# Last stage of a two-layer kernel: the routing weights of 48 of 64 experts spread by DMA, in four pieces a tile

## What is computed

```python
x = x + _L0_attn_ref(_layernorm(x), ...)       # selective mixing, 16 states
x = x + _L0_ffn_ref(_layernorm(x), ...)        # 9 experts, top 2
x = x + _L1_attn_ref(_layernorm(x), ...)       # 16 heads, causal, 256 tokens a row
x = x + _L1_ffn_ref(_layernorm(x), ...)        # 64 experts, top 8

def _L1_ffn_ref(x, centroids, expert_biases, Ws_up, Ws_down, W_up, W_down):
    shared = silu(xf @ Ws_up) @ Ws_down
    aff = xf @ centroids.T
    _, idx = top_k(aff + expert_biases, 8)
    w = sigmoid(take_along_axis(aff, idx, axis=1))
    w = w / (sum(w, axis=-1, keepdims=True) + 1e-08)
    cw = zeros((T, 64)).at[arange(T)[:, None], idx].add(w)
    h = silu(einsum('td,edf->etf', xf, W_up))     # 64 experts, 128 -> 64
    y = einsum('etf,efd->etd', h, W_down)         # 64 -> 128
    return shared + einsum('etd,te->td', y, cw)
```

## Time and profile before

| | us |
|---|---|
| median of 3 runs | 1128.03 (1126.86 to 1128.64) |
| the profiled execution | 1126.31 |
| its span | 1124.5 |
| TensorE busy | 981.0 (87%) |
| VectorE busy | 846.1 (75%) |
| ScalarE busy | 723.8 (64%) |
| GpSimd busy | 439.8 (39%) |

### The profile page before, as it was taken

One profiled execution on the slowest core, in us unless ns is written; L12 is line 12 of the kernel. 1 busy time (PEld: TensorE's weight loads), 2 busy tenths in 40 slices (PEclk: granted clock), 3 DMA queues, 4 the chain that ended last, 5 costly groups with the idle time before them and its releaser, 6 DMA issues.

```text
span 1124.5 us, 20697 instructions
## 1 busy us (share of the span) xinstructions
PE 981.0 (87%) x6164; PEld 779.5 (69%) x6164; DVE 846.1 (75%) x1938; ACT 723.8 (64%) x1416; POOL 439.8 (39%) x503
## 2 busy tenths in 40 slices
PE   5665089999658999999999989999999999999998
PEld 3444079999536777776776667777777677777776
DVE  4865577777568888888887667878787768787865
ACT  4543045555347778778777667777777667777775
POOL 0266750000156556555553303333333333333343
PEclk9555589999869999999999989999999999999999
DMA  9011122222211101101010013241414140505050
GB/s 251 18 45 46 65 58 65 64 66 66 68 28 24 34 20 29 29 23 36 20 30 11 1 43 86 50 87 44 92 36 101 35 103 12 124 12 125 12 124 10
DMA packets 59749, 61.68 MB, mean 55 GB/s; under 512 B 15973, under 2 KB 54022, under 8 KB 57606
## 3 DMA queue, kind: packets, MB, share of 16 engines
q1 hardware_dynamic: 54976, 52.02, 19.4%
q0 software_dynamic: 4096, 8.40, 2.4%
q10 hardware_dynamic: 582, 0.09, 0.0%
HBM read 45.73 MB, written 14.75 MB: 54 GB/s over the span
## 4 chain that ended last, share of the span: by engine, by line
PE 74%; DVE 12%; ACT 5%; issue 5%; POOL 1%; DMA 1%; SPq 1%; DVEq 0%; POOLq 0%; ACTq 0%
PE ps L2070 5%; PE ps L2048 5%; PE ps L2050 4%; PE ps L2049 4%; PE ps L2072 4%; PE ps L2071 4%; PE ps L1848 4%; PE ps L1791 3%; PE ps L1911 3%; PE ps L2057 3%; PE ps L1866 3%; PE ps L1894 3%; PE ps L1872 2%; PE ps L1770 2%; PE ps L1769 2%
## 5 line engine op out<-in xcount | busy, mean ns | idle before, releaser
L741 POOL TENSOR_TENSOR hl<-h,hh 128x512 fp32r<-128x512 f32 x128 | 165.7, 1294 | 309.0 <-ACT hh L1017 309.0
L1017 ACT ACTIVATE hh<-h 128x512 fp32r<-128x512 f32 (+1 forms) x264 | 165.0, 625 | 17.4 <-DVE h L1634 16.1
L1534 DVE TENSOR_REDUCE nm<-ps 128x4 f32<-128x512 f32 (+1 forms) x128 | 116.3, 951 | 35.6 <-PE ps L1894 33.7
L1634 DVE TENSOR_TENSOR h<-sg,ps 128x512 f32<-128x512 f32 x160 | 108.2, 676 | 39.5 <-ACT sg L1005 37.9
L1005 ACT ACTIVATE sg<-ps 128x512 f32<-128x512 f32 x160 | 95.7, 598 | 54.4 <-PE ps L2050 54.2
L645 POOL DMA_INDIRECT yg<-ys,gps x64 | 63.0, 984 | 168.6 <-issue 158.1
L2070 PE MATMUL ps<-hh,wh 128*128 128x512 f32 x256 | 103.6, 405 | 18.0 <-DVE hl L1641 17.0
L2048 PE MATMUL ps<-xh,wh 128*128 128x512 f32 x256 | 105.8, 413 | 0.0
L1634 DVE TENSOR_TENSOR h<-ps,cwB 128x512 f32<-128x512 f32 x96 | 65.8, 685 | 50.2 <-ACT ps L1005 45.7
L1641 DVE TENSOR_TENSOR hl<-h,hh 128x512 fp32r<-128x512 f32 (+1 forms) x136 | 93.0, 684 | 13.6 <-ACT hh L1017 13.6
L2050 PE MATMUL ps<-xh,wl 128*128 128x512 f32 x256 | 102.7, 401 | 0.0
(11 more groups left out here) (320 smaller groups left out, 2741.1 us busy)
## 6 DMA issues: line engine op xcount, KB each, us to landing
cwB<-cwd SPq DMA_DIRECT2D x16, 1536.0 KB, 10.8
xb<-xs SPq DMA_DIRECT2D x72, 64.0 KB, 1.8
ys<-yb SPq DMA_DIRECT2D x72, 64.0 KB, 1.6
cwd<-cwS SPq DMA_DIRECT2D x32, 96.0 KB
x_res<-in_L_attn_x_dram SPq DMA_DIRECT2D x4, 512.0 KB, 9.1
wst<-in_L_ffn_W_up_dram SPq DMA_DIRECT2D x32, 64.0 KB, 2.2
wst<-in_L_ffn_W_down_dram SPq DMA_DIRECT2D x32, 64.0 KB, 1.9
out_dram<-y SPq DMA_DIRECT2D x8, 256.0 KB, 4.9
```

The source lines that it names most:

```text
L741: pool.tensor_tensor(hl4[:, u % 3, :], h4[:, u % 3, :], hh4[:, u % 3, :].bitcast(F32), op=ALU.subtract).then_inc(u_hlp, 1)
L1017: act.activation(hh4[r, u % 3, :], h4[r, u % 3, :], ACT.Copy).then_inc(u_hh, 1)
L1534: ins = dve.tensor_reduce(nm[:, u, 4 * g:4 * g + 4], o, axis=AX.X, op=ALU.max, negate=True)
L1634: dve.tensor_tensor(h4[:, u % 3, :], first, second, op=ALU.mult).then_inc(u_h, 1)
```

## The change

- `NS` goes from 20 to 8: units 1 to 8 have their weights spread by TensorE, and units 9 to 32, all of them, by DMA (`NB` = 24, so 48 experts).
- The 24 units come in four pieces of six (`NPC`, `G`). `cwB` has three buffers (`NBUF`), and the fourth piece goes into the first buffer again, once unit 14 has used it (`rows_again`).
- Each row has four copies in `cwd` instead of eight (`CWR`). A tile's writes are still four transfers, now one for each copy, each of all 48 rows.
- From unit 9 on the up projections rotate over five banks, 0 to 4 (`up_bank`, `wait_bank`).
- The experts are taken in order (`pair_of` and `unit_of` are gone). VectorE's `weights` step writes 48 rows in piece order instead of 24.
- To make room, the attention's `wuT` is placed and loaded later, with the shared weights, and some semaphores of GpSimd's attention work become one. GpSimd's `selr` has 16 columns of experts instead of 40.

```diff
-        NS = 20
+        NS = 8
         NB = NP2 - NS
         EP, EB = 2 * NS, 2 * NB
-        HB = 32
-        CWR = 8
-        cwd = nc.dram_tensor("cwd", [2, 2, 2, CWR, NB // 2 * TT], F32).ap()
+        HB = 64
+        CWR = 4
+        NPC, NBUF = 4, 3
+        G = NB // NPC
+        cwd = nc.dram_tensor("cwd", [2, NPC, 2, CWR, G * TT], F32).ap()
...
-        cwB = sb("cwB", [P, NB, TT], F32)
+        cwB = sb("cwB", [P, NBUF, G, TT], F32)
...
         def broadcast_unit(u):
-            return u > 8 and u % 2 == 1
+            return u > NS
...
+        def rows_of_unit(u):
+            piece, j = divmod(u - NS - 1, G)
+            return piece, piece % NBUF, j
...
+        def up_bank(u):
+            return u % 3 if u <= NS else (u - NS - 1) % 5
+
+        def spread_bank(u):
+            return 3 + u % 2
...
-            G = NB // 2
+            def load_rows(t, piece):
+                sp_.dma_start(cwB[:, piece % NBUF, :, :].rearrange("p u t -> p (u t)"),
+                              cwd[t % 2, piece].rearrange("h r x -> (h r) x").unsqueeze(1).broadcast_to(
+                                  [2 * CWR, F2 // CWR, G * TT])).then_inc(rows_in[piece % NBUF], 16)
 
             def spread_rows(t):
                 sp_.wait_ge(d_cw, t + 1)
-                for g in range(2):
-                    for half in range(2):
-                        sp_.dma_start(cwd[t % 2, g, half].rearrange("r (e t) -> e r t", t=TT),
-                                      cwS[half * NB + g * G:half * NB + (g + 1) * G, :].unsqueeze(1).broadcast_to(
-                                          [G, CWR, TT])).then_inc(rows_out, 16)
-                sp_.wait_ge(rows_out, 64 * (t + 1))
-                for g in range(2):
-                    if t == 0 and g == 1:
-                        sp_.wait_ge(c_F6, B + 1)
+                for r in range(CWR):
+                    sp_.dma_start(cwd[t % 2, :, :, r, :].rearrange("k h x -> (k h) x"), cwS[0:EB, :]).then_inc(rows_out, 16)
+                sp_.wait_ge(rows_out, 16 * CWR * (t + 1))
+                for piece in range(NBUF):
+                    if t == 0 and piece == 1:
+                        sp_.wait_ge(c_PV, 4 * B)
+                        sp_.wait_ge(d_const, 2)
+                    if t == 0 and piece == 2:
+                        sp_.wait_ge(c_F3, B)
                     if t > 0:
-                        sp_.wait_ge(u_h, (t - 1) * NP2 + 9 + 2 * (g * G + G - 1))
-                    sp_.dma_start(cwB[:, g * G:(g + 1) * G, :].rearrange("p u t -> p (u t)"),
-                                  cwd[t % 2, g].rearrange("h r x -> (h r) x").unsqueeze(1).broadcast_to(
-                                      [2 * CWR, F2 // CWR, G * TT])).then_inc(rows_in[g], 16)
+                        last = max(k for k in range(NPC) if k % NBUF == piece)
+                        sp_.wait_ge(u_h, (t - 1) * NP2 + NS + (last + 1) * G)
+                    load_rows(t, piece)
+
+            def rows_again(t):
+                for piece in range(NBUF, NPC):
+                    sp_.wait_ge(u_h, t * NP2 + NS + (piece - NBUF + 1) * G)
+                    load_rows(t, piece)
 
             spread_rows(0)
             for t in range(T // TT):
                 if t > 0:
                     sp_.wait_ge(u_y, t)
                     sp_.dma_start(out_tok[:, (t - 1) * SUB:t * SUB, :], y4[:, (t - 1) % 2, :, :]).then_inc(o_out[(t - 1) % 2], 16)
+                rows_again(t)
                 if t + 1 < T // TT:
                     spread_rows(t + 1)
```

More of the change, by code:

```diff
@@ L257, in bass_two_layers @@
         ooT = sb2("ooT", [P, 2, P], F32)
+        wuT = sb2("wuT", [P, D], F32)
         attn.close()
@@ L347, in bass_two_layers @@
         dve_ln = sem("dve_ln")
-        pool_w = sem("pool_w")
+        pool_w = sem("pool_links")
         u_hlp = sem("e_hl_pool")
         rows_out = sem("weight_rows_out")
-        rows_in = [sem("weight_rows_in0"), sem("weight_rows_in1")]
-        pool_h, u_sg0 = sem("pool_h"), sem("e_silu_shared")
+        rows_in = [sem(f"weight_rows_in{i}") for i in range(NBUF)]
+        u_sg0 = sem("e_silu_shared")
         def weight_piece(piece):
@@ L386, in broadcast_unit, with rows_loaded, wait_bank @@
         def broadcast_unit(u):
-            return u > 8 and u % 2 == 1
[L390 to L398, removed]
+            return u > NS
+        def rows_of_unit(u):
+            piece, j = divmod(u - NS - 1, G)
+            return piece, piece % NBUF, j
+        def rows_loaded(piece, t):
+            twice = piece % NBUF + NBUF < NPC
+            return 16 * (2 * t + 1 + piece // NBUF if twice else t + 1)
+        def up_bank(u):
+            return u % 3 if u <= NS else (u - NS - 1) % 5
+        def spread_bank(u):
+            return 3 + u % 2
+        BANKS_USED = [(use, u, bank_(u)) for u in range(NP2 + 1) for use, bank_, there in (
+            ("up", up_bank, True), ("spread", spread_bank, 0 < u <= NS)) if there]
+        def wait_bank(eng, t, use, u):
+            n = BANKS_USED.index((use, u, up_bank(u) if use == "up" else spread_bank(u)))
+            earlier = [(a, v, t) for a, v, k in BANKS_USED[:n] if k == BANKS_USED[n][2]]
+            if not earlier:
+                if isinstance(t, int) and t == 0:
+                    return
+                earlier = [(a, v, t - 1) for a, v, k in BANKS_USED if k == BANKS_USED[n][2]]
+            a, v, t_of = earlier[-1]
+            if v == 0:
+                eng.wait_ge(u_sg0, t_of + 1)
+            elif a == "spread" or broadcast_unit(v):
+                eng.wait_ge(u_h, t_of * NP2 + v)
+            else:
+                eng.wait_ge(u_sg, t_of * NP2 + v)
         def x4_bank(n):
@@ L505, in _ @@
                 sp_.wait_ge(ys_out[u], 16 * (NBLK // 4 + 1))
+            sp_.dma_start(wuT[:, :], WuT).then_inc(sh_in, 16)
             sp_.dma_start(shf[:, 0:F2], Ws_up).then_inc(sh_in, 16)
@@ L998, in e_silu @@
                 r = slice(0, F2 if u == 0 else P)
+                up = bank[up_bank(u)]
                 if u == 0:
@@ L1624, in e_h @@
                 if broadcast_unit(u):
-                    j = pair_of(u) - NS
-                    first, second = bank[u % 3][:, :], cwB[:, j, :]
-                    if j % (NB // 2) == 0:
-                        dve.wait_ge(rows_in[j // (NB // 2)], t * 16 + 16)
-                else:
-                    dve.wait_ge(u_cw, t * NS + pair_of(u) + 1)
-                    first, second = sg4[:, u % 3, :], bank[3 + pair_of(u) % 2][:, :]
+                    piece, buf, j = rows_of_unit(u)
+                    first, second = bank[up_bank(u)], cwB[:, buf, j, :]
+                    if j == 0:
+                        dve.wait_ge(rows_in[buf], rows_loaded(piece, t))
+                else:
+                    dve.wait_ge(u_cw, t * NS + u)
+                    first, second = sg4[:, u % 3, :], bank[spread_bank(u)]
                 if u >= 3 or not (isinstance(t, int) and t == 0):
@@ L2017, in pe_turn @@
                 if F:
+                    if i == 1:
+                        pe.wait_ge(sh_in, 16 * 5)
                     if M:
@@ L2051, in e_up @@
                 if u > 0 and not broadcast_unit(u):
-                    i = pair_of(u)
-                    if i >= 2:
-                        pe.wait_ge(u_h, t * NP2 + unit_of(i - 2))
-                    elif not first:
-                        pe.wait_ge(u_h, (t - 1) * NP2 + unit_of(NS + i - 2))
-                    pe.matmul(bank[3 + i % 2][:, :], selr[:, 2 * i:2 * i + 2, :].rearrange("p e f -> p (e f)"), cwT[:, p, :],
+                    wait_bank(pe, t, "spread", u)
+                    pe.matmul(bank[spread_bank(u)][:, :], selr[:, 2 * u - 2:2 * u, :].rearrange("p e f -> p (e f)"), cwT[:, p, :],
                               start=True, stop=True).then_inc(u_cw, 1)
```

62 lines of the change are left out of this document (26 added, 36 removed).

## The result

The changed kernel takes **1250.98 us** (median of four runs, 1250.28 to 1251.49) against 1127.44 for the kernel before (four runs, 1124.31 to 1128.64). The ratio is 1.11, 95% interval 1.1076 to 1.1124: 124 us more, where 149 more were forecast. The profiled execution took 1250.28 us, with a span of 1248.5.

What follows compares the result with a forecast made beforehand. The chain of four loads was to bound each tile: 7.0 + 2.2 + 59.2 + 1.0 + 5.8 = 75.2 us instead of 56. Seven periods, the last tile and the remainder gave 1277 us, range 1165 to 1305.

Steps and rivals of the forecast that it cites:

- I take the smaller side: 8 engines for the new loads: Loads of weight rows in the last stage: the smaller outermost count, 8 on the source, limits the DMA engines, 16 before.
- Rival 1: Loads still use all 16 engines because the destination's 128 decides; the 12 us are gained, 1116 us; chance 0.13.
- 14.8 us: Time of each of a tile's four loads on eight engines, twice the 7.4 us before.
- Rival 2: Loads on eight engines, each faster than now: 12 us a load, 1187 us; chance 0.09 for prices from 9.7 to 13.5.
- write to first load: I take 7.0, bounds 6 and 8: SP's queue in each tile: from the first write to the first load 7.0 us, 8.0 before.
- 2.2 us ahead of the first load's data: Start of each tile's chain of loads: 2.2 us beyond the load's own time before the first one lands.
- from unit 27 to the next first write: 5.8 us: End of each tile's chain: from the fourth piece's first unit to the next tile's first write, 5.8 us.
- TensorE's clock may add some: Stretch from unit 27 to the next first write: a lower TensorE clock could lengthen it by some 2 us a tile.
- rival 3: TensorE's half clock becomes the bound in the pieces: 17 us a piece, 84 us a tile, about 1345 us; chance 0.02.
- 12 us, if the loads hide as before: Gain from twelve fewer matmuls a tile: 1.3 us in each of seven tiles plus 2.8 us in the last.
- The banks add nothing: Up projections on five banks: no part of the gain, since they wait for silu only 2.5 us over the stage.
- Buffers don't stop it: Loads of pieces 1 to 3 reuse buffers already freed by units up to 32, 20 and 26 of the tile before.

Runs made afterwards that it cites:

- after_cwr8: The changed kernel with CWR 8 instead of 4 and nothing else: 1132.29 us, ratio 0.9917 to the kernel before.

## Why the prediction was right

The sign, the mechanism and the place were right; the time was 26 us too high, inside the range given and just below the forecast's own of 1255 to 1305. (The terms named for that range reach down to 1277 - 8 - 6 = 1263 only, so its lower end was 8 us wider than its reasons.) By the steps, for the tile from 1024.75 to 1096.55:

- **"I take the smaller side: 8 engines for the new loads."** Right: share 0.51, and eight packets under way; four with a count of 4. Rival 1, that the destination's 128 decides, fell. The rule of the Trainium skill, page "DMA: Bandwidth & Descriptors", section "Why a DMA increments its semaphore by 16 and not by 1", which counts both access patterns, agrees with the three shares of the loads and with their packets, 4, 8 and 16 at a time.
- **"14.8 us" a load.** Slightly high: the products that wait for the four loads start 14.2, 14.5 and 14.7 apart, with the store in between. The three later loads and the store were put at 3 x 14.8 + 1.0 = 45.4 us and took 43.4. Rival 2 fell too: a packet of 12 KB takes 0.881 us on average over this stage, and 0.891 in the kernel before with sixteen engines. That is 1% faster, not the quarter that its 1187 us needed.
- **"write to first load: I take 7.0, bounds 6 and 8."** This is the term that was mis-sized most: 4.7 us, outside its bounds. I had scaled the backlog by engines and taken "SP's issues alone" at the old 4.5 us. But the issues themselves got cheaper, 2.67 us for four (0.67 each, 1.14 before), and the last write landed 2.1 us after its issue had ended where it had taken 3.5. Nor was the share 0.5 as foretold, but 0.35, at 104 GB/s in place of 63. Eight engines were at work all the same: the four writes end with 32 packets of 4 bytes, the old four with 24, six each. A share alone is no sure reading of the number of engines for these small writes; that 0.33 had matched six was partly luck.
- **2.2 us ahead of the first load's data.** Unit 9 starts 16.9 us after the issue, 17.0 foretold. If this load took 14.5 us like the later ones, 2.4 us were ahead of it, so the two terms miss a little in opposite directions.
- **"from unit 27 to the next first write: 5.8 us".** 6.7: up to 1095 the clock is granted 0.64 over 4.8 us, as "TensorE's clock may add some" had left open. TensorE had stood idle for 4.07 us until 1091.17. The lower level is left again within the piece, so rival 3 (1345 us) fell: the stretch of the third piece, with its gaps, has 0.88 (1075 to 1089), not 0.5.

```profile
1091.17 0.79 PE L2101 MATMUL ps<-hh,wh 128*128 128x512 f32 x1 [4.07 <-DVE hl L1680]
...
1093.05 0.63 PE L2084 MATMUL ps<-xl,wh 128*128 128x512 f32 x1
1093.47 0.63 PE L2085 MATMUL ps<-xh,wl 128*128 128x512 f32 x1
...
1095.63 0.40 PE L2085 MATMUL ps<-xh,wl 128*128 128x512 f32 x1
1095.87 0.39 PE L2101 MATMUL ps<-hh,wh 128*128 128x512 f32 x1
```

In this timeline of TensorE starts lie 0.42 us apart at first and 0.24 at the end.

The sum: -2.3 (writes), -0.1, -2.0 (loads and store), +0.9 (clock) is -3.5 us a tile, and seven tiles at the mean period of 71.9 against 75.2 are 23 us. The first write came 1.4 us later than foretold. In the last tile unit 27 comes 63.6 us after the first write (1167.23 to 1230.83), 69.4 foretold for its landing, and the end 17.7 us after unit 27, 15 foretold, at a clock of 0.89 in that tile. Together -23 + 1.4 - 5.8 + 2.7 = -25 us, which is the miss of the span (1248.5 for 1273). The last microsecond of the 26 is the step from the profiled execution to the median, 0.7 us where 1.7 had been taken over from the kernel before.

Of the signs foretold, waits for `cwB` came four times a tile as said, 17.1 us where some 20 were foretold. TensorE was busy for 57.4 us of the middle tile, not some 50.

**"12 us, if the loads hide as before".** 9.5 us (ratio 0.9917): on average a middle tile gained 57.11 - 55.98 = 1.13 us (1.3 foretold), and the last tile 62.07 - 60.00 = 2.07 (2.8). That 1.13 is near 1.3 is luck. More than half of what seven tiles gained comes from one, the fifth: 61.76 us in the kernel before (888.34 to 950.10, clock 0.94) and 57.10 in `after_cwr8` (clock 1.00). The six others gained 0.55 us each, and so do tiles compared at a clock of 1.00, 0.6 to 0.7. The reason given beside the number was wrong as well: VectorE does not bound most of units 10 to 30. Why twelve matmuls, 2.8 us, bring only some 0.6 us in an ordinary middle tile stays open.

**"The banks add nothing"** held (0.9913 against 0.9917). **"Buffers don't stop it"** held: the fourth load was issued at 1054.72, once unit 14 was done, before the third had landed.

## What to carry to other kernels

Before a transfer is re-cut, look at the outermost count of both its sides: here 8 in place of 16 on the source alone halved the engines, and doubled the time of a load whose size had not changed. Give the chain of transfers its own sum, issues, landing of the writes and every load in its queue, and compare it with the tile: a DMA share of 0.43 over the tile looked like room and was the bound. And the same number has two ends: more copies made the loads faster and the writes slower, so that 8 was best among 4, 8 and 16.

## What was not expected of the hardware

- **A load can be twice as fast on the same 16 engines.** With 16 copies (outermost count 32 on the source) a load of 1536 KB took 3.7 us, some 425 GB/s; with 8 copies 7.4 us at a share of 1.00. Both have 16 packets under way; one of 12 KB takes 0.46 us in most cases with 16 copies, and mostly 0.77 to 0.97 with 8. So in the second case the engines are busy by the records and yet at half the rate that they can have. Two things change together: an engine reads two rows instead of one, and a row, still of 12 KB, is read by 4 partitions instead of 8. Neither explains it alone: with `CWR = 2` an engine reads one row for 32 partitions, and in the second load of most tiles its packets take only some 0.5 us too. What sets the pace was not tried apart and stays open.
- **The price of an issue on SP follows the form of the transfer.** Four writes of 6 rows x 2, 4, 8 and 16 copies take 1.30, 1.91, 4.54 and 7.13 us of SP, up to 1.78 each; a write of 48 rows takes 0.67.
- **Fewer engines need not be faster each**: going from 16 to 8 changed nothing (0.891 and 0.896 us for a packet), while with 4 a part of the loads got faster (0.629 on average).
